# High and low halves of v side by side: one product of 64 columns per head in a linear-attention block

## What is computed

```python
scores = einsum('bhtd,bhsd,hts->bhts', qi, ki, mask)
intra  = einsum('bhts,bhsd->bhtd', scores, vi)
cross  = einsum('bhtd,ht,bhde->bhte', qi, lam_t, S)
o      = scale * (intra + cross)
kv     = einsum('bhtd,ht,bhte->bhde', ki, lam_rev, vi)
S      = lam_T * S + kv
```

## Time and profile before

| | |
|---|---|
| median of 3 runs | 1431.73 us (1431.1 to 1432.38) |
| the profiled execution | 1431.59 us, its span 1429.9 us |
| PE busy | 1366.5 us (96%) |
| DVE busy | 931.6 us (65%) |
| ACT busy | 479.0 us (34%) |
| mean granted TensorE clock | 0.992 of full speed |

### The profile page before, as it was taken

The page is one execution under the profiler, slowest core; times in us unless marked ns, Lnnn a source line. Parts: engine busy times, 40 slices in busy tenths (PEclk is TensorE's granted clock), DMA queues, the critical chain, the costliest instruction groups (busy, mean ns, idle before and its releaser), DMA issues.

```text
span 1429.9 us, 24260 instructions
## 1 busy us (share of the span) xinstructions
PE 1366.5 (96%) x8924; PEld 736.9 (52%) x8924; DVE 931.6 (65%) x1899; ACT 479.0 (34%) x877; POOL 64.2 (4%) x95
## 2 busy tenths in 40 slices
PE   4798789999999999999999999999999999999999
PEld 2354444555545554555545555455555555455554
DVE  6687776556665567656675567655666557755667
ACT  7755532323322323323223233232232332322322
POOL 5110000000000000000000000000000000000000
PEclk9999999999999999999999999999999999999999
DMA  7132224211251112611153112511126111361115
GB/s 287 59 126 82 82 47 91 77 31 45 60 134 30 30 45 60 147 32 36 32 103 97 32 43 56 127 54 30 45 59 134 32 28 45 75 132 31 44 31 118
DMA packets 200193, 101.95 MB, mean 71 GB/s; under 512 B 135584, under 2 KB 184736, under 8 KB 198432
## 3 DMA queue, kind: packets, MB, share of 16 engines
q1 hardware_dynamic: 199808, 100.45, 27.9%
q10 hardware_dynamic: 288, 0.01, 0.0%
HBM read 35.40 MB, written 8.39 MB: 31 GB/s over the span
## 4 chain that ended last, share of the span: by engine, by line
PE 83%; DVE 8%; ACT 3%; issue 2%; SPq 1%; DMA 1%; POOL 0%; ACTq 0%; DVEq 0%
PE bank L445 81%; PE bank L487 2%; DVE wg_lo L1183 1%; SPq L827 1%; DMA k_stack<-k_parts 1%; DVE xin L785 1%; DVE stage L647 1%; DVE sm L685 1%; ACT wg_lo L1033 1%; DVE wu_lo L1183 0%; DVE kl L695 0%; DVE sg L800 0%; DVE wd_lo L1183 0%; DVE arena L646 0%; DVE sm_lo L646 0%
## 5 line engine op out<-in xcount | busy, mean ns | idle before, releaser
L445 PE MATMUL bank<-wd_hi,arena 128*128 128x512 f16 x1024 | 318.7, 380 | 1.2 <-DVE wd_lo L1183 1.2
L445 PE MATMUL bank<-xt,wg_hi 128*128 128x512 f16 x1024 | 307.9, 382 | 5.2 <-issue 5.0
L445 PE MATMUL bank<-xt,wu_hi 128*128 128x512 f16 x1024 | 304.8, 379 | 5.3 <-DVE sg L800 4.7
L445 PE MATMUL bank<-xt,wg_lo 128*128 128x512 f16 x512 | 196.0, 383 | 0.0
L445 PE MATMUL bank<-wd_lo,arena 128*128 128x512 f16 x512 | 194.8, 380 | 0.0
L445 PE MATMUL bank<-xt,wu_lo 128*128 128x512 f16 x512 | 194.0, 379 | 0.0
L800 DVE SCALAR_TENSOR_TENSOR sg<-bank,small,sg 128x512 f32<-128x512 f32 x128 | 95.8, 749 | 130.5 <-PE bank L445 130.3
L634 ACT ACTIVATE arena<-sg 128x512 f16<-128x512 f32 x128 | 80.6, 629 | 296.5 <-DVE sg L800 296.5
L753 DVE SCALAR_TENSOR_TENSOR arena<-bank,small,arena 128x512 f32<-128x512 f32 x160 | 119.7, 748 | 85.1 <-PE bank L445 84.8
L445 PEld LDWEIGHTS bank<-wd_hi,arena 128*128 128x128 f16 x1024 | 100.5, 98 | 118.8 <-issue 2.8
L445 PEld LDWEIGHTS bank<-xt,wu_hi 128*128 128x128 f16 x1024 | 98.4, 98 | 114.4 <-issue 4.6
(11 more groups left out here) (186 smaller groups left out, 1613.8 us busy)
## 6 DMA issues: line engine op xcount, KB each, us to landing
q_stack<-q_parts SPq DMA_DIRECT2D x192, 64.0 KB, 2.2
k_stack<-k_parts SPq DMA_DIRECT2D x192, 64.0 KB, 2.2
xin<-x SPq DMA_DIRECT2D x34, 256.0 KB, 4.5
arena<-x SPq DMA_DIRECT2D x8, 1024.0 KB, 5.6
out<-arena SPq DMA_DIRECT2D x32, 256.0 KB, 3.4
stage<-gate_t SPq DMA_DIRECT2D x4, 1024.0 KB, 5.0
stage<-up_t SPq DMA_DIRECT2D x4, 1024.0 KB, 6.0
stage<-down_t SPq DMA_DIRECT2D x4, 1024.0 KB, 5.1
```

Source lines behind the costliest of these rows:

```text
L445: last = e.matmul(dst, a, b, start=start and n == 0, stop=stop and n == len(lhs) - 1)
```

## The change

The two halves of v now lie side by side per head, in one tensor `v` with the shape `[P, 2, HEADS, 2, HD]`. So one matmul of 64 columns gives `sm_hi` with both halves, the product with v's high half in one group of 32 columns of `b_o` and that with its low half in another. `sm_lo` with the high half is added to the first group by a matmul of 32 columns, and the cross product too. The bank now holds two sums that have to be added: ACT copies the one of the low halves into `o`, DVE adds the other to it, and a further DVE instruction scales the result in place. The cross product has moved behind the heads' matmuls and writes 4 groups of 32 columns with gaps of 32. KV reads v, and the evictions of V write it, in groups of 32 with gaps. `O s+1 0` waits for the add (`OSUM`) in place of the scaling.

```diff
-    v = [sb(f"v_{n}", [P, 2, D], F16) for n in ("hi", "lo")]
+    v = sb("v", [P, 2, HEADS, 2, HD], F16)
...
+    def o_parts(c):
+        return b_o[:, HALF * c:HALF * (c + 1)].rearrange("p (h n d) -> p h n d", h=HPG, n=2)
+    def o_both():
+        return b_o[:, :].rearrange("p (c h n d) -> p c h n d", c=2, h=HPG, n=2)
+    def o_slice(j):
+        return o[:, :, P * j:P * (j + 1)].rearrange("p c (h d) -> p c h d", h=HPG)
...  PE, KV
-                                [v[n][:, c, f] for n in (0, 1, 0)])
+                                [v[:, c, HPG * j:HPG * (j + 1), n, :] for n in (0, 1, 0)])
...  PE, O
             if c == 0:
-                e.wait_ge(ve["OUT"].sem, ve["OUT"].at(blk, s))
+                e.wait_ge(ve["OSUM"].sem, ve["OSUM"].at(blk, s))
                 cross = state[:, a, j, :]
             else:
+                cross = state1[:, :]
+            both = o_parts(c)
+            for h in range(HPG):
+                vh = v[:, c, HPG * j + h, :, :]
+                e.matmul(both[:, h, :, :], smp[0][:, h, :], vh, start=h == 0, stop=False)
+                e.matmul(both[:, h, 0, :], smp[1][:, h, :], vh[:, 0, :], start=False, stop=False)
+            if c:
                 e.wait_ge(ve["S1"].sem, ve["S1"].at(blk, s + 1))
-                cross = state1[:, :]
-            products(b_o[:, P * c:P * (c + 1)], [ql[:, s % 2, P * c:P * (c + 1)]], [cross], stop=False)
-            for h in range(HPG):
-                f = slice(P * j + HD * h, P * j + HD * (h + 1))
-                last = products(b_o[:, P * c + HD * h:P * c + HD * (h + 1)],
-                                [smp[0][:, h, :], smp[0][:, h, :], smp[1][:, h, :]],
-                                [v[n][:, c, f] for n in (0, 1, 0)], start=False, stop=h == HPG - 1)
+            last = products(both[:, :, 0, :], [ql[:, s % 2, P * c:P * (c + 1)]], [cross], start=False)
             last.then_inc(pe["O"].sem, 1)
...  ACT, O s 1 (the waits for ZT and the tables moved here from DVE)
+            e.wait_ge(pe["O"].sem, pe["O"].at(blk, 2 * s + 2))
+            e.activation(o_slice(j), o_both()[:, :, :, 1, :], ACT.Copy).then_inc(ac["O"].sem, 1)
...  DVE, O s 1
-            e.wait_ge(pe["O"].sem, pe["O"].at(blk, 2 * s + 2))
-            e.tensor_tensor(o[:, :, P * j:P * (j + 1)].rearrange("p c (h d) -> p c h d", h=HPG),
-                            b_o[:, 0:HALF].rearrange("p (c h d) -> p c h d", c=2, h=HPG),
-                            head[:, 3, HPG * j:HPG * (j + 1)].unsqueeze(1).unsqueeze(3).to_broadcast([P, 2, HPG, HD]),
+            mine = o_slice(j)
+            e.wait_ge(ac["O"].sem, ac["O"].at(blk, s + 1))
+            e.tensor_tensor(mine, o_both()[:, :, :, 0, :], mine, ALU.add).then_inc(ve["OSUM"].sem, 1)
+            e.wait_ge(ve["OSUM"].sem, ve["OSUM"].at(blk, s + 1))
+            e.tensor_tensor(mine, mine, head[:, 3, HPG * j:HPG * (j + 1)].unsqueeze(1).unsqueeze(3).to_broadcast([P, 2, HPG, HD]),
                             ALU.mult).then_inc(ve["OUT"].sem, 1)
```

More of the change, by code:

```diff
@@ L328, in build @@
     ac = {k: C("act_" + k, n, b) for k, n, b in (
-        ("V", 4, 0), ("Q", 8, 0), ("K", 8, 0), ("KT", 8, 0), ("SM", 16, 0), ("SQ", 4, 0), ("Z", 4, 0),
+        ("V", 4, 0), ("Q", 8, 0), ("K", 8, 0), ("KT", 8, 0), ("SM", 16, 0), ("O", 8, 0), ("SQ", 4, 0), ("Z", 4, 0),
         ("TX", 4, 4), ("TH", 4, 4), ("SILU", 16, 1), ("GH", 16, 0))}
@@ L499, in tensor_item @@
             for c in range(2):
-                t, f = slice(P * c, P * (c + 1)), slice(P * j, P * (j + 1))
+                t = slice(P * c, P * (c + 1))
                 last = products(bank[:, t], [kt[0][:, t], kt[0][:, t], kt[1][:, t]],
-                                [v[n][:, c, f] for n in (0, 1, 0)])
+                                [v[:, c, HPG * j:HPG * (j + 1), n, :] for n in (0, 1, 0)])
             last.then_inc(pe["KV"].sem, 1)
@@ L572, in scalar_item @@
             e.wait_ge(pe["V"].sem, pe["V"].at(blk, it[1] + 1))
-            e.activation(v[0][:, it[1] % 2, :], bank_of(it, blk)[:, :], ACT.Copy, scale=QKV_SCALE).then_inc(ac["V"].sem, 1)
+            e.activation(v[:, it[1] % 2, :, 0, :], bank_of(it, blk)[:, :].rearrange("p (h d) -> p h d", h=HEADS), ACT.Copy, scale=QKV_SCALE).then_inc(ac["V"].sem, 1)
         elif kind in ("Q", "K"):
@@ L590, in scalar_item @@
             e.activation(smp[0][:, :, :], sm[:, :, :], ACT.Copy).then_inc(ac["SM"].sem, 1)
+        elif kind == "O":
+            _, s, c = it
+            if c == 0:
+                return
+            a, j = divmod(s, GROUPS)
+            e.wait_ge(pe["O"].sem, pe["O"].at(blk, 2 * s + 2))
+            if isinstance(blk, int):
+                e.wait_ge(pe["ZT"].sem, pe["ZT"].at(blk, 2 * a))
+            if s == 0 and isinstance(blk, int):
+                e.wait_ge(s_tern, KT + 1)
+            e.activation(o_slice(j), o_both()[:, :, :, 1, :], ACT.Copy).then_inc(ac["O"].sem, 1)
         elif kind == "NA":
@@ L655, in vector_item @@
             c = it[1] % 2
-            lo(v[1][:, c, :], bank_of(it, blk)[:, :], QKV_SCALE, v[0][:, c, :], ac["V"], it[1] + 1).then_inc(ve["V"].sem, 1)
+            lo(v[:, c, :, 1, :], bank_of(it, blk)[:, :].rearrange("p (h d) -> p h d", h=HEADS), QKV_SCALE, v[:, c, :, 0, :], ac["V"], it[1] + 1).then_inc(ve["V"].sem, 1)
         elif kind == "Q":
@@ L1088, in _ @@
                           pm4[:, :].unsqueeze(2).to_broadcast([P, HPG, HD]))
-            for name in ("Q", "K", "KT", "KVM", "SM", "OUT", "SUM", "Z", "Y", "GT", "GL"):
+            for name in ("Q", "K", "KT", "KVM", "SM", "OSUM", "SUM", "Z", "Y", "GT", "GL"):
                 e.sem_inc(ve[name].sem, ve[name].before)
```

## The result

| | before | after |
|---|---|---|
| median of 16 runs | 1431.33 us (1429.51 to 1433.28) | 1428.37 us (1425.84 to 1430.51) |
| the profiled execution's span | 1429.9 us | 1427.2 us |

The ratio is 0.9979, with a 95% interval of 0.9971 to 0.9986: 0.21% faster, 2.96 us, where 1428.9 was forecast.

A forecast was written before the change was run, and what follows sets the result against it. PE was taken to bound the loop; 0.06 us saved in seven of eight `O s 0` a turn makes 0.41 us, over 7 turns 2.9; 1431.6 - 2.8 = 1428.8, stated as 1428.9 us, range 1421 to 1436.

The forecast's parts named there:

- What bounds the kernel: Loop: PE, busy 167.77 of 168.70 us a turn, sets the time; outside its waits, time off its stream is saved.
- A matmul of 64 columns: Products with v: 0.029 us each by the column slope, bounds 0.026 and 0.056; saves 0.09 us an item.
- The cross product loses its cover: Behind 32 columns its weight loads show, 0.33 us; `O s 0` falls from 0.64 to 0.58, `O s 1` 0.75 to 0.74.
- rival (a): Cross product behind 32 columns costs 0.22 us, its loads hidden: 8 us more gained, 1421 us; chance 0.13.
- Seven of eight steps count: Loop: step 6's saving becomes a longer PE wait, leaving 0.41 us a turn, 2.9 us in 7 turns.
- Block 0 put at nothing: Before the loop: no net change, between a gain of 0.5 us and a loss of 1.5 us.
- The evictions cost nothing: DVE and ACT: some 29 and 24 us more work, `UL` 1.15 us later, but PE does not wait.
- Rival (c): Evictions reach PE through `UL`, `Silu` and the next G: 5.6 us lost, 1434.5 us; chance 0.15.
- the 1.4 us of further delay: From `Silu`'s end at 717.9 to the next G at 719.32: 1.4 us of cover left after the later `UL`.
- the mask 0.9 us late: DVE's mask behind `UL` starts 0.9 us late, at 717.9, and its chain by as much; costed at nothing.
- Gaps in the operands cost nothing: KV's reads and the products' writes in runs of 32 cost PE nothing; upper bound 19 us in the loop.
- Rival (b): Matmuls with gaps are slower: KV doubled gives 19 us, 1448 us; a tenth more gives 1431; chance 0.10.

The follow-up runs named there:

- experiment 1: Kernel before, with only the cross product moved behind its twelve products of 32 columns: 1437.06 us (ratio 1.0039).
- experiment 2: Changed kernel, with the cross product held back until behind the first matmul of the next wide group: 1419.82 us (ratio 0.9925).
- experiment 3: Kernel before (twelve products of 32 columns, one eviction), with the cross product held back behind the next wide group's first matmul: 1428.85 us (ratio 0.9981).
- experiment 4: Changed kernel, with one DVE instruction in place of ACT's copy, the add and the scaling, leaving out v's low half: 1428.50 us (ratio 0.9984).
- experiment 6: Changed kernel, with six more ACT copies, each behind the one before, ahead of DVE's add: 1456.51 us (ratio 1.0178).
- experiments 7 to 9: Changed kernel with gaps after every element in v and the bank (1440.11 us), in v alone (1429.27 us), in the bank alone (1437.96 us).

## Why the prediction was right

- **What bounds the kernel.** Right: PE's stream sets the loop's time. 49 items `O s 0` that count, at 0.055 us each, are 2.7 us, and the two profiled spans differ by 2.7 (1429.9 to 1427.2). Experiments 1 to 3 came out within 0.7 us of sums made in the same way. The sum on record subtracts 2.8 where 0.41 us in 7 turns are 2.9; the slip is 0.1 us.
- **A matmul of 64 columns, taken as 0.029 us from the slope.** It measured 0.0286 on average (the step from a wide to a narrow one). An item's products went from 0.304 to 0.222 us, 0.082 less where 0.09 was read from rounded starts. If the cross product stays as it is, the wide products bring 9.0 to 9.2 us (experiments 1 to 3), for 98 x 0.09 = 8.8. That this fits so well is in part luck: 98 x 0.082 are 8.0, and in experiments 2 and 3 the rest lies in block 0, which the sum put at nothing.
- **The cross product loses its cover, 0.33 us behind a matmul of 32 columns.** Right at both kinds of item, 0.58 and 0.74 us, and shown by moving it alone (experiment 1, +6.2 us where 5.7 was expected) and by giving its cover back (experiment 2, 11.0 us under its before where the changed kernel is 3.0 under its own: 8.0 us, with 8.3 expected). So rival (a), loads hidden behind a short matmul, is out. Its 1421 us can be reached, but by the order of the matmuls: experiment 2 took 1419.82.
- **Seven of eight steps count.** Right: the waits of step 6 grew, and the chain from U to the scores stayed at 12.05 us.
- **Block 0 put at nothing.** It measured 0.06 us less. On the way PE was 1.44 us ahead at `O 2 1`, at 199.52 in place of 200.96, but the scores at 205.08 and 205.15 start within 0.1 us of each other, after a wait for `k_stack` of 2.27 us in place of 0.81. So what PE is ahead ends in this wait. In the single traces of the variants block 0 ends between 243.68 and 252.52 us, and between 243.68 and 246.59 without experiment 6; so the 0.06 of one pair of executions is in line with a cost of zero and doesn't prove it.
- **The evictions cost nothing.** Right (experiment 4), with 1.07 us of delay where 1.15 was worked out. Rival (c) exists beyond the cover: the 1.4 us of further delay that I named at `UL` held (0.8 us more cost nothing, 2.4 made PE wait for `Silu` by up to 1.0). I overlooked the other place that gives way at 2.4, the adds into `y` ahead of the next turn (experiment 6). One sum was wrong: I had the mask 0.9 us late, but DVE had stood idle for 0.88 us ahead of it in the trace of before, and that had to come off first. It starts 0.53 us after the scores do, where it was 0.42 (716.51 to 716.93), so it was late by 0.11 us. DVE's and ACT's busy times rose by 25.3 and 18.0 us, for 29 and 24 in the prediction; the copy and the add last 371 and 420 ns each, as forecast, but records of neighbours overlap (the copy starts at 714.02, the one ahead ends at 714.11).
- **Gaps in the operands cost nothing.** Right for this layout; the reason given, that the array and not the reading sets the pace, holds for reads. KV's reads with a gap after every float16 cost 0.002 us each. Rival (b) was looked for in these reads, and it lies in writes, at gaps after every element (experiments 7 to 9). The rule of the Trainium skill that any non-contiguous pattern slows a matmul significantly (PSUM — Partial Sum Buffer, Specifications (TRN2)) holds here for the products with v when they write with a gap after each float32 (0.085 us for 0.055), and neither for their runs of 32 nor for the cross product.

## What to carry to other kernels

In these traces a float32 matmul's weight loads begin when the matmul ahead has started. Behind 256 or 512 columns the product adds 0.22 us, and behind 32 it costs 0.08 us more than that. So when narrow matmuls are merged or moved, look at what each float32 product then stands behind: here some 6 of the 9 us that the wide products bring went back at that point. An order that puts one wide matmul between them got these back, and with them the 2.0 us that the kernel before lost behind KV; the one new wait that shows, for `sm_lo`, is 0.2 us a turn. And a saving counts only in stretches where PE never waits on a chain that starts ahead of it: add up steps between such waits, not over the whole program.

## What the runs showed of the hardware

- Start to start, matmuls of 32, 64, 128, 256 and 512 columns took 0.026, 0.029, 0.056, 0.109 and 0.216 us here: between 32 and 64 columns the width is nearly free.
- Writing a bank with a gap after each float32 cost 0.03 us for a pair of a 64- and a 32-column product (0.085 for 0.055). The float32 cross product, which writes so as well there, kept its 0.30 us from its own start to the next item's. The delay shows behind the 32 columns (0.056 for 0.027), not behind the 64 (0.029); whether the 64 columns' writes cause it can't be told from starts, and both records last 221 ns.
- The float32 cross product took 0.33 us from the start of the matmul ahead to that of the next behind 32, 128 or 256 columns, and 0.44 behind 512.
- V's eviction (128x512) with a gap after each float16 took ACT 743 ns in place of 597, and DVE 732 in place of 692.
